# Attention scores in a mixture-of-experts block: q and k in two f32r parts on half the rows, in place of three bf16 parts on 96

## The chip, the cores and the metric

The kernel runs on one core of one Trainium2 chip. The metric is device time in microseconds, of which the median over the runs is compared. The core's engines are called PE (matrix multiplication), DVE (vector), ACT (scalar, activations), POOL (GpSimd) and SP (it only issues transfers here). SBUF has 128 partitions, and PSUM has banks of 512 f32 values in each partition.

## What is computed

One transformer layer with normalisation behind each part, for 8 sequences of 512 tokens and 256 channels: causal attention with 16 heads of 16 channels, then an expert layer in which each of 8 experts picks 129 tokens of each sequence.

```python
def proj(W):
    return jnp.einsum('btc,oc->bto', x, W).reshape(b, t, h, hd).transpose(0, 2, 1, 3) * inv_sqrt_c
k = proj(W_key)
q = proj(W_query)
v = proj(W_value)
scores = jnp.einsum('bhqd,bhkd->bhqk', q, k) * hd ** (-0.5)
causal = jnp.tril(jnp.ones((t, t), dtype=bool))
scores = jnp.where(causal, scores, -jnp.inf)
weight = jax.nn.softmax(scores, axis=-1)
out = jnp.einsum('bhqk,bhkd->bhqd', weight, v)
...
x = _layernorm(x + _L0_attn_ref(x, ...), axis=-1)
x = _layernorm(x + _L0_ffn_ref(x, ...), axis=-1)
```

The picks of the experts hang on small differences between scores, so the attention is computed nearly to f32. All inputs and outputs are f32.

## The kernel before

`attention` does the first half and `experts` the second; the change touches `attention` and the order of the weight columns in `kernel`. Each engine walks through the same list, `steps()`, and does the entries that are its own; semaphores keep the engines together. The list has 40 steps for a sequence (four quarters `g` of ten steps `k`). Each step has one `st` unit, and the `nat` units of a head group are spread over the ten steps of a quarter, three quarters ahead. In steps 4 to 7 of a quarter an `av` entry follows. The table `STAGES` puts the other work at fixed steps: `qk` (four tiles of q and k, for the sequence after next), `stack`, `nmcut` and `nm`, `v`, `onorm`, `ot`, `proj`, and the normalisation.

Scores are computed twice. The first pass, `nat` (L712), has queries in the partitions and finds each row's maximum: PE writes a bank `n_ps` (ring of 3), and DVE adds the causal mask and reduces it in one operation (L569). The second pass, `st` (L698), has keys in the partitions: PE writes `st_ps` (ring of 2) with the maximum already subtracted, ACT takes the exponential into `pt` (L485), POOL zeroes what the mask hides (L425), and `av` (L741) multiplies by v for four heads, each in its own 32 columns of the array.

To keep f32 accuracy with bf16 operands, q and k are each written as three bf16 parts that add up to the value. A score is then six products, stacked along the contraction: part `K_PARTS[i]` of k meets part `Q_PARTS[i]` of q in rows 16 i to 16 i + 15, so that 96 rows of the array (`KQ`) hold six products of 16 channels. For the second pass three rows more (`KM` = 99) hold ones on the side of k and the three parts of the negative maximum on the side of q.

The parts are made and stacked in this way. PE makes a tile of q or k (L758, f32r, six matmuls of 512 columns). ACT writes the first part (L510) and an f32 copy (L511); POOL makes the other parts with three subtractions (L434 to L436), or DVE for the first sequence (L580 to L582). SP writes the three parts to DRAM, 128 KB each (`part_d`, L362), and, once all are there, reads them into the stacks `kst` and `qst` in 12 transfers for each half of the heads (L373), since each block of 16 rows takes one. The maxima are cut into three parts by DVE (`nmcut`, L599 to L602), turned by PE (L786), copied by ACT (L523) and put into the three rows by a transfer that ACT issues (L525).

The stacks use the memory of the experts' first weights, and the parts that of the raw weights, so the trace calls them `w_parts` and `w_raw`.

## Time and profile before

| | |
|---|---|
| median of 3 runs | 932.88 us (932.07 to 934.78) |
| profiled execution | 932.33 us, span 930.6 us, mean granted TensorE clock 0.956 |
| first matmul of the experts' part, by the chain | about 483 us |
| one sequence in the middle of the attention part | 50.3 us |

The rows in the section below are read as follows. A row of the busy table has the stretch, its length, then for each engine the busy time in it and the count of instructions, then the granted clock (1.00 is 2.4 GHz), the share of DMA time and GB/s. A row of the timeline or the chain has start and duration in microseconds, engine, line and operation; "x8" behind it counts merged instructions. The duration of a matmul includes its way through the array, so what it costs the next one is the distance from start to start. One plain f32 matmul is two instructions, one f32r or bf16 matmul is one. "99x384" is 99 rows by 384 columns; "99x384 bf16 x2" in the timeline is a unit of 384 and 128 columns. PEld is the loading of the stationary operand.

### The profile page before, as it was taken

What the parts mean: (1) busy time and instruction counts of PE and PEld (TensorE: products, weight loads), DVE (VectorE), ACT (ScalarE), POOL (GpSimd) and SP (SyncE); (2) the same over time, 40 slices, a digit from 0 to 9 for tenths busy, and PEclk for the clock granted to TensorE, in tenths of its full rate; (3) what the DMA queues carried; (4) which work ended last, traced back from release to release, by engine and by line L of the source; (5) the groups of instructions that cost most, each with busy time, mean ns of one, the idle gap of its engine ahead of it and who ended that gap; (6) DMA issues with size and microseconds to landing.
All of it is one profiled execution on the core that took longest, in us unless ns stands there. A gap on an engine that the chain in (4) does not pass through costs nothing.

```text
span 930.6 us, 17149 instructions
## 1 busy us (share of the span) xinstructions
PE 822.0 (88%) x5876; PEld 616.8 (66%) x5876; DVE 604.5 (65%) x2059; ACT 532.7 (57%) x1042; POOL 472.9 (51%) x642
## 2 busy tenths in 40 slices
PE   4668999999999999988739779999999999999990
PEld 3434445454545454434339769999999999999990
DVE  4358778878788788899656863556455454646454
ACT  2226666767585767666728333656565655655555
POOL 6336666656656565332577317454443443535343
PEclk9778999999999999999979899999999999999995
DMA  4999677868586958620133404334334252513158
GB/s 139 165 151 159 103 149 124 168 93 163 112 157 120 150 108 151 157 70 3 64 108 114 121 13 69 81 92 89 76 55 124 46 138 35 143 30 54 27 137 259
DMA packets 89990, 100.52 MB, mean 108 GB/s; under 512 B 8624, under 2 KB 83376, under 8 KB 89776
## 3 DMA queue, kind: packets, MB, share of 16 engines
q1 hardware_dynamic: 72448, 77.92, 40.0%
q0 software_dynamic: 12800, 16.92, 11.2%
q10 hardware_dynamic: 4656, 4.59, 1.5%
q8 instruction: 47, 0.77, 0.4%
q14 instruction: 39, 0.32, 0.1%
HBM read 65.38 MB, written 33.62 MB: 106 GB/s over the span
## 4 chain that ended last, share of the span: by engine, by line
PE 66%; DVE 14%; ACT 5%; issue 5%; DMA 5%; POOL 2%; SPq 1%; ACTq 0%; POOLq 0%; DVEq 0%
PE y_ps L1303 19%; PE h_ps L1289 19%; PE av_ps L741 7%; DVE n_ps L569 5%; PE st_ps L709 5%; PE n_ps L724 4%; DMA part_d<-w_raw 3%; PE stage_ps L758 3%; PE stage_ps L766 3%; PE stage_ps L800 2%; PE tp_ps L1262 2%; ACT pt L485 1%; DVE nmax L569 1%; ACT res L533 1%; PE stage_ps L791 1%
## 5 line engine op out<-in xcount | busy, mean ns | idle before, releaser
L569 DVE CUSTOM_DVE_ANT_0 n_ps<-n_ps,tri 128x512 f32<-128x512 f32 (+3 forms) x512 | 238.6, 518 | 85.0 <-PE n_ps L724 83.2
L485 ACT ACTIVATE pt<-st_ps 128x512 f32<-128x512 f32 x320 | 184.3, 602 | 66.1 <-PE st_ps L709 50.8
L1303 PE MATMUL y_ps<-w_parts,h_hi 128*128 128x256 f32 (+1 forms) x1152 | 215.2, 281 | 0.6 <-DVE w_parts L1214 0.6
L1131 ACT ACTIVATE g<-h_ps,b 128x384 f32<-128x384 f32 (+1 forms) x192 | 104.3, 543 | 169.5 <-PE h_ps L1289 169.5
L1289 PE MATMUL h_ps<-tt_hi,w_parts 128*128 128x384 f32 (+1 forms) x768 | 173.1, 328 | 22.0 <-DVE tt_lo L1177 14.1
L1103 POOL DMA_INDIRECT acc<-y,tok_no x64 | 103.2, 1613 | 146.4 <-DVE y L1238 140.0
L1303 PEld LDWEIGHTS y_ps<-w_parts,h_hi 128*128 128x128 f32 (+1 forms) x1152 | 172.8, 178 | 4.2 <-ACT h_hi L1136 0.9
L425 POOL TENSOR_SCALAR_AFFINE_SELECT pt<-pt 128x256 f32<-128x256 f32 (+1 forms) x320 | 110.7, 363 | 116.6 <-ACT pt L485 115.9
L1224 DVE TENSOR_TENSOR h_lo<-g,h_hi 128x384 fp32r<-128x384 f32 (+1 forms) x176 | 90.2, 513 | 121.2 <-ACT h_hi L1136 121.0
L1303 PE MATMUL y_ps<-w_parts,h_lo 128*128 128x256 f32 (+1 forms) x576 | 161.6, 281 | 0.0
L1289 PEld LDWEIGHTS h_ps<-tt_hi,w_parts 128*128 128x128 f32 x768 | 127.9, 191 | 22.9 <-ACT tt_hi L1122 14.3
L709 PE MATMUL st_ps<-w_parts 99*128 99x512 bf16 (+3 forms) x512 | 125.2, 306 | 15.1 <-ACT pt L485 13.4
L724 PE MATMUL n_ps<-w_parts 96*128 96x512 bf16 (+3 forms) x512 | 126.2, 310 | 10.7 <-DVE nmax L569 6.9
L1303 PEld LDWEIGHTS y_ps<-w_parts,h_lo 128*128 128x128 f32 (+1 forms) x576 | 102.1, 177 | 2.1
L709 PEld LDWEIGHTS st_ps<-w_parts 99*128 99x128 bf16 x512 | 41.4, 98 | 86.8 <-ACT pt L485 56.8
L1136 ACT ACTIVATE h_hi<-g 128x384 fp32r<-128x384 f32 (+1 forms) x192 | 94.4, 492 | 7.4
L741 PE MATMUL av_ps<-pt,vaug 128*32 128x512 f32 (+3 forms) x1024 | 97.0, 453 | 0.0
L1289 PE MATMUL h_ps<-tt_lo,w_parts 128*128 128x384 f32 (+1 forms) x384 | 92.9, 323 | 0.0
L1076 POOL DMA_INDIRECT tok<-x,tok_no x58 | 58.5, 1009 | 40.0 <-issue 40.0
L569 DVE DVE_READ_ACCUMULATOR2_ANT nmax<- 128x1 f32 x512 | 71.9, 140 | 0.0
L724 PEld LDWEIGHTS n_ps<-w_parts 96*128 96x128 bf16 x512 | 44.4, 99 | 40.9 <-DVE nmax L569 25.4
L1235 DVE TENSOR_TENSOR y<-y_ps,b 128x256 f32<-128x256 f32 (+1 forms) x72 | 30.3, 421 | 58.6 <-PE y_ps L1303 54.6
...
## 6 DMA issues: line engine op xcount, KB each, us to landing
...
```

The source lines that it names most:

```text
L425: nc.gpsimd.affine_select(out=x, in_=x, compare_op=ALU.is_ge, fill=0.0, base=0, pattern=[[0, len(tiles)], [1, P]], channel_multiplier=-1). ...
L485: nc.scalar.activation(pt[:, slot % PT_RING, n % UP, :], st_ps[at % ST_RING][:, :], ACT.Exp, scale=S_SCALE).then_inc(exp_done, 1)
L569: ins = nc.vector.tensor_tensor_reduce(out=src[:, h, :], in0=src[:, h, :], in1=mask, scale=-1.0, scalar=-BIG_NEG, op0=ALU.add, op1=ALU.min ...
L709: ins = nc.tensor.matmul(st_ps[at % ST_RING][:, c:c + T - kb * P], kst[0:KM, b % 2, h, kb * P:(kb + 1) * P], qst[0:KM, b % 2, h, kb * P:T] ...
L724: ins = nc.tensor.matmul(bank[:, j * w:(j + 1) * w], qst[0:KQ, b % 2, h, qb * P:(qb + 1) * P], kst[0:KQ, b % 2, h, 0:w], start=True, stop= ...
L741: ins = nc.tensor.matmul(av_ps[VW * j:VW * (j + 1), n * P:T], vaug[:, seq % 3, n, h, :], pt[:, (seq * PAIRS + h // 2) % PT_RING, u, c:c + ...
L1103: nc.gpsimd.indirect_dma_start(acc_d[0:reach(j), :], bass.IndirectOffsetOnAxis(ap=choice(e, j), axis=0), y[0:rows_of(j), j, :], None, comp ...
L1131: nc.scalar.activation(g[:, at % G_RING, 0:cols], h_ps[at % H_RING][:, 0:cols], ACT.Gelu, bias=b1[:, e, n:n + 1]).then_inc(g_done, 1)
L1136: nc.scalar.activation(h_hi[:, q % 2, n, 0:cols], g[:, at % G_RING, 0:cols], ACT.Copy).then_inc(g_hi, 1)
L1224: nc.vector.tensor_tensor(h_lo[:, q % 2, n, 0:cols], g[:, at % G_RING, 0:cols], h_hi[:, q % 2, n, 0:cols].bitcast(F32), ALU.subtract).then ...
L1289: ins = nc.tensor.matmul(h_ps[at % H_RING][:, 0:cols], w[e % 2][:, k, units], x[:, q % TOK_RING, k, 0:cols], start=i == 0, stop=i == len(t ...
L1303: ins = nc.tensor.matmul(y_ps[at % Y_RING][0:rows, 0:C], x[:, q % 2, m, toks], w[e % 2][:, m, :], start=i == 0, stop=i == len(terms) - 1)
```

## The change

The three bf16 parts become two f32r parts, and six products become three: k in parts (0, 1, 0) against q in parts (0, 0, 1). That is 48 rows, or 50 with the two rows for the maximum. Heads are placed in two groups of rows, 0 to 49 and 64 to 113: pair n (heads 2n and 2n + 1) goes to group n mod 2. The columns of the q and k weights are put in the order in which a tile of 128 channels falls into the two groups (`HEAD_ORDER`). The `nat` units are cut anew: a pair has five units of 512 columns at most, as `st` has, and the pair is the neighbour (`slot ^ 1`) of the one that `st` has at the same place in the list, so that the two lie in different groups.

```diff
-K_PARTS = (0, 0, 1, 1, 0, 2)
-Q_PARTS = (0, 1, 0, 1, 2, 0)
-
-BLOCKS = len(K_PARTS) + len(Q_PARTS)
+K_PARTS = (0, 1, 0)
+Q_PARTS = (0, 0, 1)
+
+GROUP = P // 2
+BLOCKS = 2 * (len(K_PARTS) + len(Q_PARTS))
 KQ = len(K_PARTS) * D
-KM = KQ + 3
+KM = KQ + 2
+
+
+def place_of(h):
+
+    return h // 2 % 2, h // 4 * 2 + h % 2
+
+
+def rows_for(h, rows):
+
+    first = place_of(h)[0] * GROUP
+    return slice(first, first + rows), place_of(h)[1]
+
+
+HEAD_ORDER = [8 * n + 4 * quarter + 2 * group + h for n in range(2) for group in range(2) for quarter in range(2) for h in range(2)]
...
-N_UNITS = [(qb, h - heads + 1, heads) for h in range(H) for qb, heads in ((3, 1), (2, 1), (1, 2), (0, 4)) if (h + 1) % heads == 0]
+N_PAIR = (((0, 3, 0),), ((1, 3, 0),), ((0, 2, 0), (0, 0, 384)), ((1, 2, 0), (1, 0, 384)), ((0, 1, 0), (1, 1, 256)))
+N_UNITS = [[(2 * (slot ^ 1) + h, qb, c) for h, qb, c in unit] for slot in range(PAIRS) for unit in N_PAIR]
...
+        sp.wait_ge(ones_ready, 1)
+        for first in (0, GROUP):
+            dst = kst_b[first + KQ:first + KM, :, :, :].rearrange("p a h n -> p (a h) n")
+            sp.dma_start(dst, ones[:, :].bitcast(BF16).unsqueeze(1).to_broadcast([KM - KQ, 2 * HH, 2 * T])).then_inc(ones_in, 16)
...
-                for part in range(3):
-                    sp.dma_start(part_d[which, b % 2, part, half_, :, :], parts[:, tile % 2, part, :]).then_inc(parts_out[tile % 2], 16)
+                for part in range(2):
+                    sp.dma_start(part_d[which, b % 2, part, half_, :, :], parts[:, tile % 2, part, :].bitcast(BF16)).then_inc(parts_out[tile % 2], 16)
...
                     for at, part in enumerate(blocks):
-                        src = part_d[which, b % 2, part, n, :, :].rearrange("(h d) n -> d h n", d=D)
-                        sp.dma_start(stack[at * D:(at + 1) * D, b % 2, HH * n:HH * (n + 1), :], src).then_inc(stack_in[n][b % 2], 16)
+                        for first in (0, GROUP):
+                            src = part_d[which, b % 2, part, n, first:first + GROUP, :].rearrange("(h d) n -> d h n", d=D)
+                            sp.dma_start(stack[first + at * D:first + (at + 1) * D, b % 2, HH // 2 * n:HH // 2 * (n + 1), :],
+                                         src).then_inc(stack_in[n][b % 2], 16)
...
-                link(nc.gpsimd.tensor_tensor(qk_r[:, :], qk_f[:, tile % 2, :], parts[:, tile % 2, 0, :], ALU.subtract))
-                link(nc.gpsimd.tensor_tensor(parts[:, tile % 2, 1, :], qk_f[:, tile % 2, :], parts[:, tile % 2, 0, :], ALU.subtract))
-                nc.gpsimd.tensor_tensor(parts[:, tile % 2, 2, :], qk_r[:, :], parts[:, tile % 2, 1, :], ALU.subtract).then_inc(qk_rest, 1)
+                nc.gpsimd.tensor_tensor(parts_r[:, tile % 2, 1, :], qk_f[:, tile % 2, :], parts[:, tile % 2, 0, :], ALU.subtract).then_inc(qk_rest, 1)
...
-                act.dma_start(qst[KQ:KM, b % 2, HH * n:HH * (n + 1), :], nmt[:, :]).then_inc(rows_in, 16)
+                for group in range(2):
+                    act.dma_start(qst_b[group * GROUP + KQ:group * GROUP + KM, b % 2, HH // 2 * n:HH // 2 * (n + 1), :],
+                                  nmt[HH * group:HH * (group + 1), :].bitcast(BF16)).then_inc(rows_in, 16)
...
-                link(nc.vector.tensor_copy(nm3[:, :, 0, :], mine))
-                link(nc.vector.tensor_tensor(nmax_r[:, :, :], mine, nm3[:, :, 0, :], ALU.subtract))
-                link(nc.vector.tensor_copy(nm3[:, :, 1, :], nmax_r[:, :, :]))
-                nc.vector.tensor_tensor(nm3[:, :, 2, :], nmax_r[:, :, :], nm3[:, :, 1, :], ALU.subtract).then_inc(nm_parts, 1)
+                link(nc.vector.tensor_copy(nm2[:, :, :, 0, :].bitcast(F32R), mine))
+                nc.vector.tensor_tensor(nm2[:, :, :, 1, :].bitcast(F32R), mine, nm2[:, :, :, 0, :], ALU.subtract).then_inc(nm_parts, 1)
...
                 for hh, kb, c in ST_UNITS[u]:
-                    h = 2 * pair + hh
-                    ins = nc.tensor.matmul(st_ps[at % ST_RING][:, c:c + T - kb * P], kst[0:KM, b % 2, h, kb * P:(kb + 1) * P],
-                                           qst[0:KM, b % 2, h, kb * P:T], start=True, stop=True)
+                    rows, slot = rows_for(2 * pair + hh, KM)
+                    ins = nc.tensor.matmul(st_ps[at % ST_RING][:, c:c + T - kb * P], kst[rows, b % 2, slot, kb * P:(kb + 1) * P],
+                                           qst[rows, b % 2, slot, kb * P:T], start=True, stop=True)
...
-                for j in range(heads):
-                    h = h0 + j
-                    ins = nc.tensor.matmul(bank[:, j * w:(j + 1) * w], qst[0:KQ, b % 2, h, qb * P:(qb + 1) * P],
-                                           kst[0:KQ, b % 2, h, 0:w], start=True, stop=True)
+                for h, qb, c in N_UNITS[n]:
+                    w = (qb + 1) * P
+                    rows, slot = rows_for(h, KQ)
+                    ins = nc.tensor.matmul(n_ps[at % N_RING][:, c:c + w], qst[rows, b % 2, slot, qb * P:(qb + 1) * P],
+                                           kst[rows, b % 2, slot, 0:w], start=True, stop=True)
```

On PE the order moves a little. Where `st`, `nat`, `av` and the matmuls of `v` take turns (in steps 5 to 7 of the third quarter), it reads before (L709 `st`, L724 `nat`, L741 `av`, L766 `v`):

```order
324 L709 MATMUL st_ps<-w_parts 128x384
325 L709 MATMUL st_ps<-w_parts 128x128
326 L724 MATMUL n_ps<-w_parts 128x384
327 L741 MATMUL av_ps<-pt,vaug 32x256 x4
328 L766 MATMUL stage_ps<-w_hi,xt_hi 128x264 x2
329 L766 MATMUL stage_ps<-w_hi,xt_lo 128x264 x2
330 L766 MATMUL stage_ps<-w_lo,xt_hi 128x264 x2
331 L709 MATMUL st_ps<-w_parts 128x256 x2
332 L724 MATMUL n_ps<-w_parts 128x512
```

and after (L725 `st`, L739 `nat`, L756 `av`, L781 `v`):

```order
350 L725 MATMUL st_ps<-w_parts 128x384
351 L725 MATMUL st_ps<-w_parts 128x128
352 L739 MATMUL n_ps<-w_parts 128x512
353 L756 MATMUL av_ps<-pt,vaug 32x256 x4
354 L781 MATMUL stage_ps<-w_hi,xt_hi 128x264 x2
355 L781 MATMUL stage_ps<-w_hi,xt_lo 128x264 x2
356 L781 MATMUL stage_ps<-w_lo,xt_hi 128x264 x2
357 L725 MATMUL st_ps<-w_parts 128x256 x2
358 L739 MATMUL n_ps<-w_parts 128x384
359 L739 MATMUL n_ps<-w_parts 128x128
```

The places of all operations stay. The `nat` unit beside each `st` unit has other columns, and every step has one, where before 11 units fell on ten steps.

On POOL the tiles of q and k stand between the masks of `pt`. Before (L425 mask, L434 to L436 split):

```order
56 L425 AFFINE_SELECT pt<-pt 128x2x128 x2
57 L434 TENSOR_TENSOR w_raw<-w_raw 128x512
58 L435 TENSOR_TENSOR w_raw<-w_raw 128x512
59 L436 TENSOR_TENSOR w_raw<-w_raw 128x512
60 L425 AFFINE_SELECT pt<-pt 128x128
```

and after (L450 mask, L459 split):

```order
63 L450 AFFINE_SELECT pt<-pt 128x2x128 x2
64 L459 TENSOR_TENSOR w_raw<-w_raw 128x512
65 L450 AFFINE_SELECT pt<-pt 128x128
66 L450 AFFINE_SELECT pt<-pt 128x2x128
67 L450 AFFINE_SELECT pt<-pt 128x128
```

Two of three subtractions are gone. On ACT, where the turned maxima are stored, there stands before:

```order
68 L485 ACTIVATE pt<-st_ps 128x512 x6
69 L523 ACTIVATE nmt<-stage_ps 24x512
70 L525 DMA w_parts<-nmt 3x8x512
71 L485 ACTIVATE pt<-st_ps 128x512
72 L492 ACTIVATE xt_hi<-w_raw 128x1024
```

and after:

```order
68 L503 ACTIVATE pt<-st_ps 128x512 x6
69 L541 ACTIVATE nmt<-stage_ps 16x512
70 L544 DMA w_parts<-nmt 2x4x1024 x2
71 L503 ACTIVATE pt<-st_ps 128x512
72 L510 ACTIVATE xt_hi<-w_raw 128x1024
```

ACT issues two transfers there, one for each group of rows.

## Rows read from the trace of the kernel before

**Rows 1.** The page: busy time of each engine, and the chain by engine.

```profile
PE 822.0 (88%) x5876; PEld 616.8 (66%) x5876; DVE 604.5 (65%) x2059; ACT 532.7 (57%) x1042; POOL 472.9 (51%) x642
PE 66%; DVE 14%; ACT 5%; issue 5%; DMA 5%; POOL 2%; SPq 1%; ACTq 0%; POOLq 0%; DVEq 0%
```

**Rows 2.** Busy table of middle sequences; PE, PEld, DVE, ACT, POOL, clock, DMA share, GB/s.

```profile
194.12:244.44 50.32, 48.25 (x354) 25.53 (x353) 40.18 (x168) 34.61 (x71) 31.09 (x57) 1.00 0.77 138
294.72:345.03 50.31, 48.22 (x354) 25.52 (x353) 40.18 (x168) 34.62 (x71) 31.08 (x57) 1.00 0.73 127
```

**Rows 3.** Timeline of PE, separate steps around `av`; start, us, engine, line.

```profile
264.07 0.39 PE L709 MATMUL st_ps<-w_parts 99*128 99x384 bf16 x2
264.30 0.33 PE L724 MATMUL n_ps<-w_parts 96*128 96x384 bf16 x1
264.56 0.64 PE L741 MATMUL av_ps<-pt,vaug 128*32 128x256 f32 x8
265.13 0.39 PE L709 MATMUL st_ps<-w_parts 99*128 99x256 bf16 x2
265.36 0.38 PE L724 MATMUL n_ps<-w_parts 96*128 96x512 bf16 x1
```

**Rows 4.** Timeline of PE where steps follow each other directly.

```profile
258.96 0.39 PE L709 MATMUL st_ps<-w_parts 99*128 99x256 bf16 x2 [0.37 <-ACT pt L485]
259.25 0.39 PE L724 MATMUL n_ps<-w_parts 96*128 96x512 bf16 x1
```

**Rows 5.** Weight loads by form, 150 to 350 us: busy us, mean ns, idle before.

```profile
L724 PEld LDWEIGHTS n_ps<-w_parts 96*128 96x128 bf16 x255 | 22.0, 97 | 9.6 <-DVE nmax L569 4.6
L758 PEld LDWEIGHTS stage_ps<-xt_hi,w_hi 128*128 128x128 f32 x32 | 5.3, 189 | 2.7 <-DVE scores L617 1.3 <-ACT o_t L529 0.8
```

**Rows 6.** Timeline of PE: four f32 transposes, then a step with six `nat` matmuls.

```profile
276.66 0.60 PE L750 MATMUL stage_ps<-ident,av_sb 128*128 128x128 f32 x4
277.10 0.38 PE L709 MATMUL st_ps<-w_parts 99*128 99x384 bf16 x2
277.32 0.60 PE L724 MATMUL n_ps<-w_parts 96*128 96x256 bf16 x6
277.76 0.38 PE L709 MATMUL st_ps<-w_parts 99*128 99x512 bf16 x1
```

**Rows 7.** The chain in order of time, in the experts: f32r matmuls of 256 columns.

```profile
650.25 2.84 PE y_ps L1303 x24
```

**Rows 8.** Timeline of PE: `av` of 128 columns, then `v`.

```profile
254.37 0.43 PE L741 MATMUL av_ps<-pt,vaug 128*32 128x128 f32 x8
254.73 0.51 PE L766 MATMUL stage_ps<-w_hi,xt_hi 128*128 128x264 f32 x2
255.07 0.41 PE L766 MATMUL stage_ps<-w_hi,xt_lo 128*128 128x264 f32 x2
255.31 0.40 PE L766 MATMUL stage_ps<-w_lo,xt_hi 128*128 128x264 f32 x2
```

**Rows 9.** Timeline of ACT: the issue of the transfer of the maxima.

```profile
263.47 0.73 ACTq L525 DMA_DIRECT2D w_parts<-nmt  x1
```

**Rows 10.** Groups of DVE, 150 to 350 us: the second cast of the maxima.

```profile
L601 DVE CAST nm<-nmax_r 128x32 bf16<-128x32 f32 x8 | 5.2, 651 | 0.3
```

**Rows 11.** Waits, 150 to 350 us: us in total, times, longest.

```profile
PEld n_ps L724 <- DVE nmax L569: 4.6, 20, 0.3
```

**Rows 12.** The chain in order of time, at the start.

```profile
17.82 0.70 DVE w_raw L581
...
28.57 8.84 DMA part_d<-w_raw
...
38.73 1.18 POOL w_raw L434
```

**Rows 13.** Busy table of the first 50 us, columns as in rows 2.

```profile
0.00:50.00 50.00, 28.24 (x107) 20.41 (x107) 22.28 (x59) 11.50 (x23) 24.60 (x27) 0.86 0.79 151
```

**Rows 14.** Timeline of PE: the first `av`.

```profile
85.15 1.07 PE L741 MATMUL av_ps<-pt,vaug 128*32 128x512 f32 x8
```

77 lines of the change are left out of this document (37 added, 40 removed).

## The prediction

> **What bounds the kernel now.** I read the page first: PE is busy 88% of the span and two thirds of the chain that ended last are PE work [rows 1]. The second half of that chain is the experts (`h_ps`, `y_ps`), which the change does not touch. Then I read the four middle sequences of the attention part with the busy table by windows [rows 2]: each takes 50.3 us, with PE busy 48.2, DVE 40.2, ACT 34.6 and POOL 31.1. So PE is the bound, DVE comes next with 10 us to spare, and the clock was granted in full (1.00, the 2.4 GHz level), so durations there can be added without a correction. The timeline of PE then shows what a step of the loop costs [rows 3]: one `st` unit and one `nat` unit, 512 columns each at most, then usually something else (`av`, `v`, `qk`, `proj`, a transpose). A step's `st` unit runs 0.22 to 0.23 us and so does a `nat` unit of 512 columns: 0.42 ns a column, one column a cycle at 2.4 GHz. Forty steps of two units are 17.6 us of the 50.3.
>
> About 26 of the 40 steps of a sequence have another PE operation ahead of their `st` unit (193 such places stand in the whole program's order, over eight sequences with shorter ends). I call these **separate** steps. The other 14 follow each other directly; there `st` waits for the exponentials of ACT [rows 4] and a quicker PE would mostly wait longer. So the separate steps decide.
>
> **What the change can gain.** In the order of the new program a `st` unit of one head pair stands beside a `nat` unit of the other pair, which lies on the other half of the rows. Only neighbours in PE's order can overlap, and PE takes matmuls in order, so within a separate step it is the last `st` matmul that can run beside the first `nat` matmul. The five kinds of step, with s for one column at 0.42 ns, need at best: 512 beside 512, 0.21 us; 384, then 128 beside 512, 0.37; 256, then 256 beside 384, then 128, 0.32; 512 beside 384 and 128, 0.21; 384, then 128 beside 256 and 256, 0.37. Mean 0.30 instead of 0.44.
>
> **What loads take of it.** The operands turn from bf16 to f32r. The f32 loads of 128 columns have a mean of 189 ns where the bf16 ones have 97 [rows 5], and where short operations follow each other, four f32 transposes take 0.44 us, 0.11 each [rows 6]; six bf16 matmuls (2 x 256, 4 x 128 columns) took 0.44 right behind them [rows 6], which is their 1024 columns and nothing more, so bf16 loads never showed. The f32r matmuls of 256 columns in the experts take 2.84 us for 24, 0.118 each [rows 7], against 0.107 for the columns. A load of 128 f32r columns is thus worth up to 0.11 to 0.12 us of PE, and I take 0.11. A step has two to four loads (3.2 on average), so 0.35 us, more than the 0.30 above. With the first load out of the way, each further one 0.11 us later, the five kinds take 0.32, 0.43, 0.43, 0.32 and 0.43 us; mean 0.386, a gain of 0.054 a step. The Trainium skill, TensorE: Matmul & The Clock Gate, section LDWEIGHTS, gives columns / 1.2 ns for a load, 107 ns for 128, and no dependence on rows: half the rows would load no faster. The rows of the trace agree with that for f32, and by it the sum is the same.
>
> **What entering and leaving the half-row arrangement costs.** The trace has one change of the array's arrangement: from 128 x 128 to the four 32-column strips of `av`. There a `nat` unit of 384 columns lasts 0.26 us until `av` starts, where its columns take 0.16 [rows 3]: 0.10 us. On the way back, the first two `v` matmuls take 0.34 us behind `av` where the next two take 0.24 [rows 8]: another 0.10. No row shows a change to half the rows. Its bounds: nothing, if the next loads run under what is still streaming, as they do now between `v` and `st`; and 0.19 us, a whole f32 load [rows 5], if nothing is loaded ahead. A bf16 load that was not ahead cost 0.07 (0.29 instead of 0.22, where `st` waited for ACT [rows 4]). I take 0.13, the middle of 0.07 and 0.19, since the array's one rearrangement that the trace shows is not free. The Trainium skill, TensorEngine Tiling (Array Packing), section Key Properties, says that changing the tiling mode drains TensorE. The `av` rows agree; without a drain the sum would be that of the second case below.
>
> So a separate step costs 0.386 + 0.13 = 0.516 instead of 0.44: 26 x 0.076 = **+2.0 us** a sequence. Ten steps leave for an f32 operation over all rows (in the others `av` follows, which is paid already): 10 x 0.10 = **+1.0 us**.
>
> **The rest of a sequence.** ACT issues two transfers of the row maxima where it issued one, 0.73 us each [rows 9]. The first of the two places lies where the exponentials hold PE, so one of them is paid: **+0.7 us**; the other is under PE work. DVE loses two of the four operations of `nmcut` (the cast of 0.65 us [rows 10] and a subtraction of 0.19, for each half), some 1.7 us a sequence, and its units now come one a step instead of 11 for ten steps; PE's loads wait 4.6 us for DVE in four sequences [rows 11], so I take **-0.8 us** of the 1.15 a sequence. POOL loses two subtractions of 1.18 us (as in [rows 12]) for each of four tiles, 9.4 us a sequence, but no PE wait on POOL is long there, so nothing. The stacks take as many transfers of 128 KB as before (12 a half), in lines of 2 KB instead of 1; the parts go out as two transfers of 256 KB instead of three of 128, a third more bytes. The queue has gaps in every sequence (DMA share 0.73 to 0.77 [rows 2]), so nothing either.
>
> Sum for one sequence: 2.0 + 1.0 + 0.7 - 0.8 = **+2.9 us**. PE is the bound in about six of eight: from 95 to 388 us (293 / 50.3 = 5.8); behind that the picking rounds stand on DVE, and I count nothing there. 6 x 2.9 = +17.4 us.
>
> **The start.** The first 85 us are a chain through the parts: a tile of q or k is split (DVE 0.70 us three times for the first, POOL 1.18 three times later), written out (8.84 us from issue to landing, behind the transfers ahead of it), and read back [rows 12]. One of three subtractions stays. On the chain stand one DVE group and three POOL groups: 2 x 0.72 + 3 x 2 x 1.2 = 8.6 us go. But what is late next is the transfers, busy 0.79 of the first 50 us [rows 13], whose bytes grow. Bounds: 0 and -8.6; I take half, **-4.3 us**.
>
> **The number.** The profiled execution took 932.33 us with a span of 930.6; the median of the three runs is 932.88, so I count from 932.3 and lose nothing that matters. 932.3 + 17.4 - 4.3 = **945 us**, slower by 1.4%.
>
> **Rivals.**
> (a) *Loads go ahead of the change* (faster, a little). If entering costs nothing, a step gains 0.054: -1.4 + 0.7 - 0.8 = -1.5 a sequence, -9 in six, with the start 932.3 - 9 - 4.3 = **919 us**. For it: between `v` and `st` nothing is lost now. Against: the `av` rows. The point between this and my forecast is an entry of about 0.07 us.
> (b) *Full overlap* (faster, clearly). If loads to the idle half hide, a step takes 0.30: -0.14 x 26 = -3.6, with the other terms -3.7; six times -22, and the start: **906 us**. For it: the four strips of `av` do run together, since four heads of 256 plain f32 columns take 0.57 us [rows 3] and of 128 take 0.36 [rows 8], 0.21 for 128 columns more, which is four cycles a column once and not four times over. Against: the f32 load row. The Trainium skill, TensorE: Matmul & The Clock Gate, section Measured speedup vs the span model, has a pack of tiles take one matmul plus 4 ns for each further one: that is this case. It would end at DVE's 40 us only if it gained ten.
> (c) *Narrow f32r is slow* (slower still). Sixteen `st` and sixteen `nat` matmuls a sequence have 128 columns. No f32r row in the trace is under 256 columns. Bounds: one cycle a column as at 264 (0.24 for two [rows 8]), or four, as plain f32 in `av` (0.21 for 128 [rows 3, 8]). At four, 0.16 us more where the narrow one ends a step (two kinds in five): 0.064 x 26 = 1.7, times six +10: **955 us**.
> (d) *The halves don't run together.* Then the step stays at 0.44, pays the entry and some 0.04 for f32r (0.118 against 0.107, 3.2 times): +0.17 x 26 = 4.4, a sequence +5.3, six +32: **960 us**.
>
> **How the numbers follow.** Forecast 0.28, (a) 0.25, (b) 0.22, (c) 0.15, (d) 0.07, something else 0.03. The entry's own bounds (0.07 to 0.19) move the forecast by 9 us each way, 936 to 954. The range goes from 905, to hold (b)'s centre, to 958, past (c). A measurement of this kernel tells 0.3% (2.8 us) from no change: faster 0.44 ((a) but for a small part, and (b)), within 0.3% 0.07, slower 0.49.
>
> **What would show it.** After, a `st` unit behind `v` or `proj` starts later, by 0.1 us or more, than the last matmul before it allows; at nothing, (a) or (b). From `st` start to the next operation's start, a 512 + 512 step takes 0.32 us in the forecast and in (a), 0.21 to 0.25 in (b), 0.43 in (d). The 128-column matmuls show (c). A middle sequence would take 53 us; 46.6 is (b). The start shows in when the first `av` begins (85.15 us now [rows 14]). Wrong I would be most simply if loads of one half run fully under matmuls of the other.

## The result, and the profile after

The kernel after takes 970.92 us (median of 4 runs, 968.14 to 975.86) where the kernel before took 932.48 beside it (4 runs, 931.38 to 934.78): a ratio of 1.0415, interval 1.0361 to 1.0468. The change costs 38 us, more than the range of the prediction allowed (905 to 958). The profiled execution took 975.86 us.

The page of the kernel after: its span, its busy times, and its clock in 40 slices.

```profile
span 974.1 us, 17037 instructions
PE 874.2 (90%) x5876; PEld 663.5 (68%) x5876; DVE 587.5 (60%) x2019; ACT 533.7 (55%) x1042; POOL 405.3 (42%) x585
PEclk9557899898989899896687988999999999999996
```

The same row of the page of before reads

```profile
PEclk9778999999999999999979899999999999999995
```

PE is busy 52 us longer [rows 1], and the clock row says why to look further than at the operations. Behind a first 9 it reads 5, 5, 7, 8, then 9 with an 8 at about every second slice, then 6, 6 in the nineteenth and twentieth, where the kernel before had 9 in all slices of the middle. To place the loss I cut both executions at the same points of the program: at the start of ACT's cast `xt_hi` in the fourth and in the eighth `split`, and at the first `h_ps` matmul, with which the experts begin. The busy table by windows (columns as in [rows 2]), before:

```profile
0.00:113.57 113.57, 80.44 (x423) 48.10 (x427) 65.72 (x241) 44.84 (x94) 59.52 (x81) 0.86 0.84 147
113.57:315.09 201.52, 192.93 (x1416) 102.10 (x1408) 161.02 (x669) 138.47 (x281) 124.35 (x224) 1.00 0.75 137
315.09:482.93 167.84, 137.72 (x1019) 66.45 (x1012) 139.06 (x551) 102.29 (x193) 84.97 (x170) 0.95 0.42 89
482.93:930.60 447.67, 410.93 (x3030) 400.12 (x3030) 238.74 (x601) 247.08 (x477) 204.04 (x167) 0.96 0.40 92
```

and after:

```profile
0.00:120.61 120.61, 96.28 (x429) 62.52 (x429) 59.61 (x231) 44.95 (x93) 35.47 (x64) 0.73 0.75 153
120.61:338.77 218.16, 203.88 (x1412) 114.69 (x1408) 157.43 (x653) 139.18 (x281) 90.05 (x192) 0.91 0.65 137
338.77:525.85 187.08, 161.82 (x1017) 85.18 (x1010) 131.88 (x536) 102.21 (x193) 76.23 (x162) 0.82 0.37 82
525.85:974.10 448.25, 412.22 (x3030) 401.07 (x3030) 238.62 (x601) 247.33 (x477) 203.57 (x167) 0.96 0.40 92
```

The experts take the same time to 0.6 us. The attention part loses 7.0 us at its start, 16.6 in four middle sequences and 19.2 in its last stretch, and in each the clock is lower. The clock has two levels here, so a mean of 0.91 over 218 us is 2 x 0.09 x 218 = 39 us at the lower one. From here on **half clock** is the time at 1.2 GHz, summed as 2 x (1 - clock) over windows of 1 us. The three stretches have 31, 0 and 16 us of it before, 65, 38 and 69 us after.

The timeline of PE shows both what the change gained and what it paid. Two steps of the kernel after at full clock follow (start, us, engine, line). Behind the first, at 263.15, another step comes directly; the second is a separate one, between `v` and `av`:

```profile
263.15 0.49 PE L725 MATMUL st_ps<-w_parts 50*128 50x512 f32 x1
263.15 0.51 PE L739 MATMUL n_ps<-w_parts 48*128 48x384 f32 x2
263.48 0.34 PE L725 MATMUL st_ps<-w_parts 50*128 50x384 f32 x1
...
267.26 0.41 PE L781 MATMUL stage_ps<-w_lo,xt_hi 128*128 128x264 f32 x2
267.60 0.44 PE L725 MATMUL st_ps<-w_parts 50*128 50x384 f32 x1
267.61 0.50 PE L739 MATMUL n_ps<-w_parts 48*128 48x512 f32 x1
267.88 0.22 PE L725 MATMUL st_ps<-w_parts 50*128 50x128 f32 x1
268.03 0.64 PE L756 MATMUL av_ps<-pt,vaug 128*32 128x256 f32 x8
```

`st` and `nat` begin within 0.01 us of each other, and the next step begins 0.33 us after the first. In the second step `nat`'s only matmul starts 0.27 us ahead of `st`'s second one, so it runs beside both. The two halves do run together. The Trainium skill, TensorE: Matmul & The Clock Gate, section Measured speedup vs the span model, gives a pack one matmul plus about 4 ns for each further tile. The trace agrees on the starts (at most 0.01 us apart) and not on the length: the step takes 0.33 us, where 512 columns alone take 0.22.

A separate step of 512 beside 512 columns, from the start of `st` to that of the next operation, takes 0.43 us all the same, hardly less than before (192.24 to 192.68, 0.44 us):

```profile
204.30 0.50 PE L725 MATMUL st_ps<-w_parts 50*128 50x512 f32 x1
204.30 0.49 PE L739 MATMUL n_ps<-w_parts 48*128 48x512 f32 x1
204.73 1.16 PE L815 MATMUL stage_ps<-wp,o_t 128*128 128x264 f32 x4
```

That is 0.33 us for the step and 0.10 for leaving the half rows.

The last `v` pair, 528 columns, lasts 0.34 us until `st` starts; 0.10 us of that is the change to half the rows, since the same pair ahead of another `v` takes 0.24 [rows 8], and ahead of `st` on 99 rows it took 0.25 in the kernel before, from 255.31 to

```profile
255.56 0.39 PE L709 MATMUL st_ps<-w_parts 99*128 99x512 bf16 x1
```

And the kernel after some 20 us later, at half clock (note `qk`, line 773, whose pairs take 0.46 to 0.57 us to the next at full clock and 1.01 here):

```profile
286.00:290.00 4.00, 3.87 (x14) 2.79 (x15) 3.01 (x12) 2.21 (x4) 2.77 (x8) 0.54 0.62 175
```
```profile
288.05 1.22 PE L773 MATMUL stage_ps<-xt_hi,w_hi 128*128 128x512 f32 x2
289.06 1.05 PE L773 MATMUL stage_ps<-xt_lo,w_hi 128*128 128x512 f32 x2
```

So there were three candidates for the loss: the loads and changes of arrangement, which the forecast had counted; new waits; and the clock, which it had not counted.

### The profile page after: what moved, and what is told of

It reads as the page before. It is cut to its first block, busy times and chain, and to the rows that moved or that the text cites. A ratio compares the mean times of both kernels' runs of the same rounds, so it can differ in the third digit from the quotient of the medians.

```text
span 974.1 us, 17037 instructions
## 1 busy us (share of the span) xinstructions
PE 874.2 (90%) x5876; PEld 663.5 (68%) x5876; DVE 587.5 (60%) x2019; ACT 533.7 (55%) x1042; POOL 405.3 (42%) x585
## 4 chain that ended last, share of the span: by engine, by line
PE 78%; ACT 8%; issue 5%; DVE 3%; DMA 3%; POOL 1%; SPq 1%; ACTq 1%; POOLq 0%; DVEq 0%
PE y_ps L1318 18%; PE h_ps L1304 18%; PE st_ps L725 10%; PE av_ps L756 9%; PE stage_ps L773 6%; PE stage_ps L815 4%; PE n_ps L739 4%; ACT pt L503 3%; PE stage_ps L781 3%; PE stage_ps L765 2%; PE tp_ps L1277 2%; PE stage_ps L801 1%; PE stage_ps L806 1%; ACT res L553 1%; DMA w_parts<-part_d 1%
## 5 line engine op out<-in xcount | busy, mean ns | idle before, releaser
L450 POOL TENSOR_SCALAR_AFFINE_SELECT pt<-pt 128x256 f32<-128x256 f32 (+1 forms) x320 | 112.6, 361 | 207.5 <-ACT pt L503 205.8
L725 PE MATMUL st_ps<-w_parts 50*128 50x512 f32 (+3 forms) x512 | 163.7, 397 | 28.0 <-ACT pt L503 26.4
L1304 PE MATMUL h_ps<-tt_hi,w_parts 128*128 128x384 f32 (+1 forms) x768 | 173.4, 328 | 16.6 <-ACT tt_hi L1137 9.3
L739 PE MATMUL n_ps<-w_parts 48*128 48x512 f32 (+3 forms) x512 | 168.6, 412 | 4.0 <-DMA w_parts<-part_d 2.7
L725 PEld LDWEIGHTS st_ps<-w_parts 50*128 50x128 f32 x512 | 88.5, 204 | 118.7 <-ACT pt L503 66.0
L756 PE MATMUL av_ps<-pt,vaug 128*32 128x512 f32 (+3 forms) x1024 | 109.9, 507 | 0.0
L739 PEld LDWEIGHTS n_ps<-w_parts 48*128 48x128 f32 x512 | 92.3, 214 | 13.0 <-issue 6.7
L1304 PEld LDWEIGHTS h_ps<-tt_lo,w_parts 128*128 128x128 f32 x384 | 67.8, 192 | 0.0
```

The lines of the kernel that those rows point to most:

```text
L450: nc.gpsimd.affine_select(out=x, in_=x, compare_op=ALU.is_ge, fill=0.0, base=0, pattern=[[0, len(tiles)], [1, P]], channel_multiplier=-1). ...
L725: ins = nc.tensor.matmul(st_ps[at % ST_RING][:, c:c + T - kb * P], kst[rows, b % 2, slot, kb * P:(kb + 1) * P], qst[rows, b % 2, slot, kb ...
L739: ins = nc.tensor.matmul(n_ps[at % N_RING][:, c:c + w], qst[rows, b % 2, slot, qb * P:(qb + 1) * P], kst[rows, b % 2, slot, 0:w], start=Tr ...
L756: ins = nc.tensor.matmul(av_ps[VW * j:VW * (j + 1), n * P:T], vaug[:, seq % 3, n, h, :], pt[:, (seq * PAIRS + h // 2) % PT_RING, u, c:c + ...
L1304: ins = nc.tensor.matmul(h_ps[at % H_RING][:, 0:cols], w[e % 2][:, k, units], x[:, q % TOK_RING, k, 0:cols], start=i == 0, stop=i == len(t ...
```

## The experiments

One note ahead of the texts on record. The half-clock times in the expectations were read from the clock's record with its times counted from another zero, which lies about 11 us ahead of the span's start (11.1 in the kernel after), so each sum covers a stretch that lies 11 us too early. Those in my text and in the table are counted from the span's start, and agree with the durations of the matmuls. For four middle sequences the two readings are 34.1 and 37.5 us for the kernel after, 54.6 and 51.2 for e3, 20.5 and 17.1 for e9. No verdict turns on the difference.

Where in an execution the clock is low is known for one of each kernel, the profiled one. Its mean over the whole is known for every run, and the kernels differ by more than their runs do: 0.945 to 0.956 before, 0.894 to 0.905 after, 0.864 and 0.870 in e3, 0.917 twice in e9, 0.931 and 0.923 in e10.

### e1 and e2: without the overlap; with all rows

e1 puts the two units of a step on the same half:

```diff
-N_UNITS = [[(2 * (slot ^ 1) + h, qb, c) for h, qb, c in unit] for slot in range(PAIRS) for unit in N_PAIR]
+N_UNITS = [[(2 * slot + h, qb, c) for h, qb, c in unit] for slot in range(PAIRS) for unit in N_PAIR]
```

> The changed kernel with the nat unit taken from the same head pair as the st unit beside it, so both lie on the same half of the rows and cannot overlap; all else as in the changed kernel. In the changed kernel the clock is granted at about 0.90 in a middle sequence, where it was 1.00 before. Theory R (matmuls on half the rows hold the clock up less, whatever their order): the clock stays at 0.85 to 0.92 in the middle. Theory I (the overlap makes PE finish early and wait, and the waits let the clock fall): the clock goes back to 1.00. In both a separate step grows from 0.43 us to about 0.6, if the overlap was real, and by 25 steps a sequence at full clock gets some 4 us longer than the changed kernel's, total 985 to 1010 us under R, 960 to 980 under I.

e2 runs every score matmul over all 128 rows of the f32r stacks (the rows between and behind the groups are filled with zeros by transfers at the start):

```diff
-    return slice(first, first + rows), place_of(h)[1]
+    return slice(0, P), place_of(h)[1]
...
-                                     scale=S_SCALE).then_inc(exp_done, 1)
+                                     scale=S_SCALE * 1e-3).then_inc(exp_done, 1)
```

> The changed kernel with every score matmul over all 128 rows of the same f32r stacks: the unused rows are set to zero once at the start, the other group's head is added into each score, and the exponential's scale is a thousandth, so the attention weights come out wrong; number, width and order of all operations are the changed kernel's. No overlap, no rearrangement of the array. Theory R and theory I: the clock is 1.00 in the middle. A separate step then costs what it did before plus at most 0.05 us for f32r; a middle sequence 50 to 52 us. If f32r alone lowered the clock it would stay near 0.90. The start has 1.8 MB more to transfer, so the total is read from the middle sequences only; expected total 935 to 950 us.

e1 took 1088.63 us in its profiled run and 1111.8 in its other one, so it has no interval; the kernel before took 932.76 beside it. e2 took 962.29 us, ratio 1.0314 (1.0284 to 1.0344). Two middle sequences of e1 and one of e2, busy table, columns as above:

```profile
121.22:198.03 76.81, 75.29 (x346) 44.38 (x342) 39.84 (x163) 36.16 (x72) 22.70 (x48) 0.68 0.48 97
198.03:262.31 64.28, 63.34 (x357) 38.42 (x353) 40.34 (x163) 35.75 (x72) 22.73 (x48) 0.85 0.56 116
```
```profile
237.49:289.84 52.35, 50.80 (x353) 34.77 (x352) 39.42 (x164) 34.57 (x71) 22.53 (x48) 1.00 0.68 142
```

Without the overlap the kernel is 113 us slower than with it (1088.63 against 975.86, the profiled runs). By their mean clocks, 0.823 and 0.894, e1 has about 178 us more at half clock; at the price below that is an estimated 77 of the 113 us, and the rest is the overlap itself. The clock fell further than Theory R had it (0.68 to 0.85 in the middle, where it expected 0.85 to 0.92), and the time lies above its range.

In e1 PE is busy 98% of the time and waits for almost nothing, and yet 20 to 49 us of each sequence are at half clock: new waits are not the cause of the low clock there. In e2, with the same f32r operands and loads, the middle sequences have 1.00 again. Its sequence is 2.1 us longer than before's 50.3: that is the price of f32r, with its other edits of the sequence (the maxima in two parts, two transfers of rows), and no change to half the rows. The total missed its forecast of 935 to 950 us, mainly by the start: the middle begins at 132.73 us instead of 113.57, behind the added transfers.

The sequences of one kernel with different clocks also price the clock: (76.81 - 64.28) us for (49.0 - 19.9) us more at half clock, 0.43 us for each. By the same price a sequence of e1 would take 64.28 - 0.43 x 19.9 = 55.7 us at full clock.

### e3, e4, e9, e10: rows alone, in the kernel before

These four leave the stacks, the loads and the `nat` units of before as they are (bf16) and only read fewer rows; the products of the rows left out are missing, in e3, e9 and e10 the maximum too. The edit of e3 for both passes:

```diff
-                    ins = nc.tensor.matmul(st_ps[at % ST_RING][:, c:c + T - kb * P], kst[0:KM, b % 2, h, kb * P:(kb + 1) * P],
+                    ins = nc.tensor.matmul(st_ps[at % ST_RING][:, c:c + T - kb * P], kst[0:KQ // 2, b % 2, h, kb * P:(kb + 1) * P],
...
-                    ins = nc.tensor.matmul(bank[:, j * w:(j + 1) * w], qst[0:KQ, b % 2, h, qb * P:(qb + 1) * P],
+                    ins = nc.tensor.matmul(bank[:, j * w:(j + 1) * w], qst[0:KQ // 2, b % 2, h, qb * P:(qb + 1) * P],
```

That is rows 0 to 47 in both passes. e4 reads rows 64 to 98 for `st` and 0 to 47 for `nat`, so on opposite halves; e9 reads rows 0 to 63 in both passes, e10 rows 0 to 67.

> The kernel before (bf16, three parts) with both passes' score matmuls cut to rows 0 to 47: three of six products and the subtraction of the maximum are left out, all else is unchanged. Half the rows without f32r and without overlap. Theory R: the clock falls in the middle sequences to about 0.90 as in the changed kernel, total 955 to 980 us. Theory I: the clock stays 1.00; the cost is the rearrangement alone, some 0.1 us for each of 26 entries and 10 exits, a sequence of 52 to 54 us, total 945 to 960 us.

> The kernel before with the nat matmuls on rows 0 to 47 and the st matmuls on rows 64 to 98 (the last two products and the maximum), so that neighbours lie on opposite halves in bf16: products are left out of the scores. The overlap of the changed kernel with the quicker bf16 loads. If loads limit a step (my prediction), a separate step falls from the 0.32 of the changed kernel (to the last matmul's end) to about 0.27, since a bf16 load is 0.05 us shorter. Theory R and theory I: the clock is below 1.00, 0.85 to 0.92; total 945 to 965 us, below the changed kernel by 10 us or more through the loads.

> The kernel before (bf16) with both passes' score matmuls cut to rows 0 to 63: four of six products, no subtraction of the maximum. 64 rows still fit half of the array. Run beside the same kernel with 68 rows. With 48 rows there were 7 to 20 us a sequence at half clock. Theory R, by the count of rows: a little better than with 48 rows, 3 to 14 us a sequence at half clock, 960 to 1000 us. Theory S (the arrangement on half the array and the changes into and out of it let the clock fall, not the rows): as with 48 rows, 1000 to 1020 us.

> The same with rows 0 to 67, four more rows, which takes the matmuls over all of the array without any rearrangement; the rows that hold data are nearly as few as in the run with 64. Theory R: nearly the clock of the run with 64 rows, well below 1.00 in the middle, total within 15 us of it (the changes themselves cost 3 us a sequence). Theory S: the clock is back at 1.00 in the middle as with 96 rows, 930 to 940 us.

Measured: e3 1013.4 us, ratio 1.0862 (1.0796 to 1.0928); e4 946.63, 1.0146 (1.0117 to 1.0175); e9 976.7, 1.0464 (1.0411 to 1.0516); e10 945.76, 1.0132 (1.0038 to 1.0226). Middle sequences of e3, e4, e9 and e10 in the busy table, the one at the highest clock and the one at the lowest of each:

```profile
244.41:297.77 53.36, 51.66 (x362) 24.67 (x363) 40.78 (x168) 34.85 (x72) 31.14 (x56) 1.00 0.70 127
297.77:360.81 63.04, 61.24 (x352) 27.53 (x344) 41.03 (x168) 34.79 (x72) 31.30 (x56) 0.81 0.61 112
```
```profile
216.75:268.83 52.08, 47.83 (x346) 22.89 (x344) 40.00 (x167) 34.55 (x71) 31.02 (x56) 0.90 0.75 133
268.83:319.06 50.23, 46.80 (x364) 22.31 (x363) 40.95 (x169) 34.54 (x71) 30.97 (x56) 0.97 0.73 138
```
```profile
120.65:177.43 56.78, 54.97 (x350) 25.60 (x346) 40.92 (x167) 34.86 (x71) 31.12 (x56) 0.91 0.66 122
231.88:285.33 53.45, 51.74 (x365) 24.73 (x363) 40.77 (x168) 34.93 (x72) 31.08 (x56) 1.00 0.72 127
```
```profile
113.30:165.18 51.88, 49.79 (x360) 26.48 (x352) 40.17 (x168) 34.61 (x71) 31.05 (x56) 0.97 0.73 130
267.61:317.89 50.28, 48.20 (x360) 25.53 (x352) 40.18 (x169) 34.61 (x71) 30.96 (x56) 1.00 0.76 138
```

Two costs come apart here. **The arrangement:** at full clock 48 and 64 rows take 53.4 us, 68 rows take 50.3, as before does with 96. Rows in number change nothing; an arrangement of half the rows costs 3.1 us a sequence, in bf16. The timeline of e9 shows a piece of it; `qk`'s last pair takes 0.55 us until `st` here and 0.46 in e2 (210.69 to 211.15), where all rows are used:

```profile
257.84 0.62 PE L758 MATMUL stage_ps<-xt_hi,w_lo 128*128 128x512 f32 x2
258.39 0.39 PE L709 MATMUL st_ps<-w_parts 64*128 64x512 bf16 x1
```
```profile
210.69 0.62 PE L777 MATMUL stage_ps<-xt_hi,w_lo 128*128 128x512 f32 x2
211.15 0.39 PE L728 MATMUL st_ps<-w_parts 128*128 128x512 f32 x1
```

**The clock:** with the work otherwise equal, half clock in four middle sequences is 0, 6.8, 17.1 and 51.2 us for 96, 68, 64 and 48 rows. PE is busy 96 to 97% of the time in all four, and the mean clocks of all their runs stand in the same order. So fewer rows lower the clock, with no f32r, no overlap and no other part of the change: from 96 to 68 rows without the cost of another arrangement (50.3 us in both), from 64 to 48 rows with the same cost. Whether the arrangement lowers the clock too is not separated. Between 64 and 68 rows it goes, and 10 us of half clock with it, where four rows are a small step.

Neither theory had the sizes. e3 lies above Theory R's 955 to 980 us, and e10 lies 31 us below e9, where R had at most 15, and above the 930 to 940 of Theory S.

The overlap in bf16 is e4 against e3: e4's four sequences, brought to full clock at 0.34 us for each us, come to 48.4 to 49.3 us, against 53.4: a gain of 4 to 5 us. The overlap gives clock back as well: e4 has 23.9 us of half clock in four sequences where e3 has 51.2, and with f32r the kernel after has 37.5 where e1 has 144.8.

### e8: half rows, loads as bf16

The kernel after, but the score matmuls read the upper 16 bits of each element of the same stacks:

```diff
-kst[rows, b % 2, slot, kb * P:(kb + 1) * P]
+kst_b[rows, b % 2, slot, 2 * kb * P + 1:2 * (kb + 1) * P:2]
```

> The changed kernel with the score matmuls reading the upper 16 bits of each f32r value as bf16 (every second bf16 element of the same stacks), so the parts lose accuracy; rows, widths, order and overlap are the changed kernel's, and only the operand type of the score matmuls differs. If the f32r load (0.11 us before the first matmul of a separate step) is what f32r costs, a separate step falls from 0.43 us to 0.37 to 0.38 and a middle sequence by 25 x 0.05 = 1.3 us plus what the clock gives. Theory R: the clock is still gated, 5 to 14 us a sequence at half clock; total 945 to 968 us. If f32r has its own part in the clock: 1.00 in the middle and 925 to 935 us.

939.73 us (4 runs), ratio 1.0072 (1.0031 to 1.0113). Two steps and their surroundings:

```profile
247.51 0.40 PE L725 MATMUL st_ps<-w_parts 50*128 50x512 bf16 x1
247.51 0.40 PE L739 MATMUL n_ps<-w_parts 48*128 48x384 bf16 x2
247.75 0.33 PE L725 MATMUL st_ps<-w_parts 50*128 50x384 bf16 x1
...
251.35 0.41 PE L781 MATMUL stage_ps<-w_lo,xt_hi 128*128 128x264 f32 x2
251.69 0.34 PE L725 MATMUL st_ps<-w_parts 50*128 50x384 bf16 x1
```

A step of 512 beside 512 columns takes 0.24 us where f32r took 0.33, so 0.09 us of an f32r load shows in each, and the overlap itself is nearly perfect (512 columns alone are 0.22). The entry behind `v` stays at 0.34 us: it does not depend on the type. With the operand type of the score matmuls alone, 31 of the 38 us are gone, and the time lies below Theory R's 945 to 968. The four middle sequences are 12.7 us shorter (205.44 against 218.16), 3.2 each. About 0.9 of that is 2.6 us less of half clock; the other 2.3 are 26 separate steps x 0.09. The start and the last stretch give more than the middle (8.4 and 16.0 us in the profiled executions), with less half clock too (41.0 us in place of 54.6 in the first 85 us, 48.1 in place of 68.9 in the last stretch); how much of that is loads and how much clock is not separated.

### e5 and e6: fillers where the steps follow each other

In the 15 direct steps of a sequence one matmul of 512 f32r columns is put ahead of `st`, on all rows (e5) or on 64 (e6); it writes a bank that the next `nat` unit overwrites.

```diff
+FILL_AT = (0, 1, 2, 4, 10, 12, 13, 14, 24, 30, 31, 32, 33, 34, 39)
...
+                    nc.tensor.matmul(n_ps[bank % N_RING][:, :], w_hi[0:P, 0, 0:P], w_hi[0:P, 0, 0:T], start=True, stop=True)
```

> The changed kernel with one more matmul of 512 columns over all 128 rows (q weights by q weights, the result is overwritten by the nat unit of the same step) ahead of the st unit in the 15 steps of a sequence whose st follows directly on nat. There PE mostly waits for ACT. Theory R (half-row matmuls do too little to hold the clock): the clock goes up in the middle, half-clock time falls from the 6.8 to 10.2 us a sequence of the changed kernel to 0 to 3.4; a middle sequence falls from 52 to 56 us to 49 to 51; total 935 to 955 us. Theory S (each change between whole and half rows lets the clock fall): the filler adds 15 changes each way, the clock falls more, total 975 to 1000 us.

> The same filler matmuls as in the run with all rows, in the same 15 places, but over 64 rows (the half on which the nat unit of that step lies). Same columns, so PE is as busy by time. If the clock asks only how busy PE is, it recovers as with all rows (0 to 3.4 us at half clock a sequence). Theory R: it recovers little, 5 us or more at half clock a sequence, and the total stays at 960 to 985 us. Theory S: no added changes, the total is that of the changed kernel, 965 to 980.

e5: 982.43 us, 1.0532 (1.0453 to 1.0611). e6: 967.6 us, 1.0373 (1.0335 to 1.041), by its time not told apart from the kernel after. e6 did what Theory R had for it. e5, which should have had a better clock than e6, did not, and missed R's 935 to 955 us; it lies in the range of Theory S, but through the columns of the fillers, as the end of this section shows. What led to them is where the clock falls. In the kernel after it fell at the same two places of nearly every middle sequence, some 47 us and some 4 us behind its start. Around 276 and 286 us the busy table reads

```profile
272.00:276.00 4.00, 2.55 (x21) 1.67 (x20) 3.48 (x15) 3.67 (x10) 1.12 (x4) 1.00 0.21 80
276.00:280.00 4.00, 4.00 (x21) 1.80 (x22) 3.07 (x17) 2.35 (x5) 1.38 (x4) 0.57 0.48 165
...
283.00:286.00 3.00, 1.85 (x19) 1.06 (x19) 1.78 (x9) 3.00 (x7) 2.23 (x2) 1.00 0.01 4
286.00:290.00 4.00, 3.87 (x14) 2.79 (x15) 3.01 (x12) 2.21 (x4) 2.77 (x8) 0.54 0.62 175
```

and the kernel before, over the same part of the program, does not fall:

```profile
257.00:261.00 4.00, 3.34 (x23) 1.55 (x21) 3.57 (x19) 4.00 (x11) 1.27 (x5) 1.00 1.13 152
...
264.80:268.00 3.20, 2.68 (x30) 1.14 (x23) 2.32 (x10) 3.20 (x7) 2.37 (x2) 1.00 0.22 75
```

Ahead of each fall PE works through direct steps at ACT's pace (ACT is busy 4.00 us of 4.00 in the kernel before and 3.67 in the kernel after). The overlapped steps are done sooner and leave PE idle 0.4 to 0.6 us between two of them: 2.55 us busy of 4 and 1.85 of 3, where before had 3.34 of 4 and 2.68 of 3.2. Over the middle, `st` waits for ACT 14.1 us instead of 6.4. The same row of e8 stands third:

```profile
PE st_ps L725 <- ACT pt L503: 14.1, 29, 0.6
```
```profile
PE st_ps L709 <- ACT pt L485: 6.4, 20, 0.4
```
```profile
PE st_ps L725 <- ACT pt L503: 18.7, 31, 0.7
```

The Trainium skill, TensorE: Matmul & The Clock Gate, section A second HAM failure mode: psum-queue depth-cycling, describes short idle times of PE between groups of matmuls that keep the clock going up and down. These rows have that form, with gaps of at most 0.6 us.

But from kernel to kernel the half clock does not follow these waits. e8 waits more than the kernel after (18.7 us) and has less of it, 27.3 us. e1 waits only 4.3 us over its four sequences and has the most, 144.8.

With the fillers the fall at 47 us is gone in both kernels; the one at 4 us stays. Half clock in four middle sequences is 27.3 us in both, from 37.5, and the mean clock of every run is above that of the kernel after (0.910 to 0.926 in e5, 0.911 to 0.921 in e6, 0.894 to 0.905 after). So work in the gaps helps. That full and half rows do the same in it speaks for the gaps and not for the rows; since e8 has the same 27.3 us without fillers, the gaps are argued as a cause and not shown. Each filler of e5 costs what it streams: its sequence at full clock took 54.41 us, 3.3 more than after's 51.1 (below), and 15 x 0.22 = 3.3.

### e11 and e12: each half filled up to 64 rows

Both put zeros into rows 48 to 61 of each half and move the maxima and the ones to rows 62 and 63; e12 also has e8's edit. `st` reads all 64 rows and `nat` 62; the expectation has the two the wrong way round.

```diff
+TOP = GROUP - 2
...
-                    rows, slot = rows_for(2 * pair + hh, KM)
+                    rows, slot = rows_for(2 * pair + hh, GROUP)
...
-                    rows, slot = rows_for(h, KQ)
+                    rows, slot = rows_for(h, TOP)
```

> The kernel after, with each half of the stacks filled up from 50 to 64 rows: the parts stay in rows 0 to 47, rows 48 to 61 hold zeros in both stacks, the maxima and the ones move to rows 62 and 63; the second pass reads rows 0 to 61, the first rows 0 to 63. The result is the same; four memsets on GpSimd at the start are added, off the chain as I read it. Theory R (the chip goes by the rows that a matmul addresses, whatever is in them): in the kernel before, cutting the rows from 96 to 68, 64 and 48 gave 0, 6.8, 20.4 and 54.6 us at half clock in the four middle sequences; so 62 and 64 rows in place of 48 and 50 take half-clock time there from 34 us to 14 or less, the last stretch before the experts from 34 us down by some 10 as well, and the time to about 950 us (940 to 958). Rival D (it goes by rows that carry data, or by the partial results that change): zero rows do nothing, half-clock time stays at 30 to 38 us in the four sequences and the time at 966 to 976 us.

> Both edits in one: 64 rows in each half filled up with zeros as in e11, and the score matmuls read the upper 16 bits of every element as bf16, as in e8 (which leaves out the lower bits of the parts). e8 alone: 939.7 us, 27.3 us at half clock in four sequences of 51.3 us. Theory R: half-clock time there falls to 10 or less, each sequence by 2 to 3 us to about 49, six sequences and a quieter start give 15 to 20 us, so 920 to 927 us, under the kernel before (933). Rival D (zero rows do nothing): 936 to 943 us as in e8.

e11: 963.7 us (4 runs), 1.0336 (1.029 to 1.0381), against 1.0415 (1.0361 to 1.0468) for the kernel after. e12: 937.62 us (10 runs), 1.0045 (1.0026 to 1.0063), against e8's 1.0072 (1.0031 to 1.0113). Half clock in four middle sequences fell from 37.5 to 20.5 us in e11, from 27.3 to 20.5 in e12. The rows that are addressed count, at least in part, though they hold only zeros. Rival D falls by e11's clock, whose mean is 0.910 to 0.914 in its four runs against 0.894 to 0.905 after; the time alone lies between the two forecasts, and e11's interval touches that of the kernel after. e12 settles nothing by itself: its time lies in the range of rival D (936 to 943), and its mean clocks (0.919 to 0.930) overlap with e8's (0.908 to 0.922). Theory R was right in direction and took too much: the clock did not come back wholly, and e12 doesn't beat the kernel before. One sequence of e12 ran at full clock throughout:

```profile
116.34:165.01 48.67, 43.65 (x352) 20.43 (x352) 38.87 (x163) 34.35 (x71) 22.42 (x48) 1.00 0.76 154
216.59:268.00 51.41, 46.47 (x352) 21.58 (x352) 38.88 (x163) 34.47 (x72) 22.44 (x48) 0.93 0.70 146
```

48.67 us is less than before's 50.3: with bf16 loads and at full clock the arrangement would gain 1.6 us a sequence. The later one, the same work, takes 2.7 us more for 6.8 us at half clock.

### e7: the new cut of the `nat` units alone

The kernel before, with only one part of the change: `nat` units by pair, five of 512 columns at most (`N_PAIR` as in the change, and each unit walked through as a list).

```diff
-N_UNITS = [(qb, h - heads + 1, heads) for h in range(H) for qb, heads in ((3, 1), (2, 1), (1, 2), (0, 4)) if (h + 1) % heads == 0]
+N_UNITS = [[(2 * slot + h, qb, c) for h, qb, c in unit] for slot in range(PAIRS) for unit in N_PAIR]
```

> The kernel before with the changed kernel's cut of the nat units alone (five of at most 512 columns for each pair, one a step; bf16, 96 rows, three parts as before). It prices the term of -0.8 us a sequence that I gave to evener units: 927 to 930 us if it holds, 932 if DVE's waits only move, with the clock at 1.00 in the middle in both.

928.95 us (6 runs, 928.15 to 930.29) beside 933.49 (10 runs): 0.9955 (0.9938 to 0.9972), a little faster than the kernel before, as expected, though by less than 0.5%. Its middle sequences take 50.0 to 50.3 us at 1.00, 0.3 us less each, so the term of -0.8 us a sequence was too large; the rest of the 4.5 us lies outside the middle. The evener units are the part of the change that is worth keeping.

## Why the prediction was wrong

At one clock the books close. Sequences of one kernel with different amounts of half clock price it: 0.34 us for each us in the kernel after ((55.84 - 52.35) / (13.7 - 3.4)), about 0.40 in e3 and e12, 0.43 in e1 and e5. Pairs with little half clock between them give 0.28 (e11) to 0.47 (e10), so the second digit of a price is not to be trusted. The four middle sequences:

| kernel | rows, type | us each | half clock us each | one at full clock |
|---|---|---|---|---|
| before | 96/99, bf16 | 50.3 to 50.6 | 0 | 50.3 |
| e10 | 68, bf16 | 50.3 to 51.9 | 0, 3.4 | 50.3 |
| e9 | 64, bf16 | 53.5 to 56.8 | 0, 3.4, 3.4, 10.2 | 53.4 |
| e3 | 48, bf16 | 53.4 to 63.0 | 0, 8.1, 19.2, 23.9 | 53.4 |
| e4 | 48 + 35 on two halves, bf16 | 50.2 to 52.1 | 3.5, 3.8, 6.6, 10.1 | about 49 |
| e2 | 128, f32r | 52.4 | 0 | 52.4 |
| e1 | 48/50, f32r, same half | 64.3 to 76.8 | 19.9, 37.9, 37.9, 49.0 | about 55.7 |
| after | 48/50, f32r, two halves | 52.4 to 55.8 | 3.4, 10.2, 10.3, 13.7 | about 51.1 |
| e8 | 48/50, bf16, two halves | 51.2 to 51.6 | 6.8 each | about 48.9 |
| e11 | 62/64, f32r, two halves | 52.4 to 53.4 | 3.4, 3.4, 6.8, 6.8 | about 51.1 |
| e12 | 62/64, bf16, two halves | 48.7 to 51.6 | 0, 6.8, 6.8, 6.8 | 48.7 |

In the column of rows, 48/50 means 48 rows in `nat` and 50 in `st`. In the last column "about" marks a value worked out with that price: 52.35 - 3.4 x 0.34 = 51.2, 50.9 at 0.43. The parts are +3.1 (arrangement: e3, e9), +2.1 (f32r: e2) and -4.6 (overlap: e1 to after; -4 to -5 from e3 to e4), together +0.6; found +0.8.

**The step that failed is the first one:** "the clock was granted in full (1.00, the 2.4 GHz level), so durations there can be added without a correction". This was true of the kernel before and was carried over to a kernel that uses half the rows, where 37.5 us of the four middle sequences were at half clock. The clock has no term in the sum, no rival and no sign of being wrong. Of the 42.9 us up to the experts, the middle's 16.6 are 4 x 0.8 = 3 at full clock and 13 by 38 us of half clock. The last stretch has 53 us more of it for 19.2 us longer, 0.36 each, the same price. The start has 34 more for 7.0 us, 0.21 each, less than the price. The experiments show that the rows bring the clock down and price it in the middle; that the whole 19.2 and 7.0 are clock is read from these prices and not shown by a run of its own. e2 comes nearest: with the same f32r operands on all rows it has 7.9 us of half clock in the last stretch and takes 168.56 us there, against 167.84 before and 187.08 after.

A second step failed with it. Of the sequences behind 388 us the prediction said "the picking rounds stand on DVE, and I count nothing there". Yet 19.2 of the 42.9 us came behind 338.77 us. From 443 to 478 us, 48 to 83 us ahead of the experts, PE of the kernel after is busy 33.63 of 35 us at half clock; over the same distance (400 to 435 us) it was busy 29.41 of 35 before. That reads as if the low clock had made PE the bound there too.

**Overlap.** "PE takes matmuls in order, so within a separate step it is the last `st` matmul that can run beside the first `nat` matmul" is wrong: `nat` starts with `st`'s first matmul and runs beside both. A step takes 0.24 us in bf16 (e8), where I had a mean of 0.30 as the best case.

**Loads.** I took 0.11 us for each further f32r load, on one chain for both halves, and so 0.386 us. Found are 0.33 and some 0.09 us over bf16: about one load shows in a step, and the others run under its matmuls. Separate steps take 0.43 us to the next operation whether they have two loads (204.30) or four (198.87 to 199.30, 256 + 256 beside 384 + 128). Rows don't make a load cheaper, as I said: 189 ns for 128 rows [rows 5], 199 and 202 ns now, over a stretch with some half clock in it:

```profile
L739 PEld LDWEIGHTS n_ps<-w_parts 48*128 48x128 f32 x233 | 39.9, 202 | 0.0
L725 PEld LDWEIGHTS st_ps<-w_parts 50*128 50x128 f32 x234 | 39.3, 199 | 54.2 <-ACT pt L503 32.0 <-issue 19.7
```

**Entering and leaving.** Taken 0.13 and 0.10, found 0.09 to 0.10 at the entry and the same on the way out: `nat` of 384 columns lasts 0.25 us until `proj` in e9 (258.62 to 258.87) and 0.16 on 68 rows in e10 (274.10 to 274.26). In a sequence that is 3.1 us where I had 26 x 0.13 + 1.0 = 4.4. That changing the arrangement isn't free was right. Together with overlap and loads the sum of a sequence came out as +2.9, found about +0.8, six of them some 12 us too much: but for the clock, the forecast would have been too high.

**The start.** The -4.3 us did not come: the first `av` starts at 87.96 instead of 85.15 [rows 14], with 54.6 us of the first 85 at half clock instead of 30.7.

**Rivals.** (b) was right that the halves run fully beside each other, wrong that the loads hide. (c) is refuted: a 128-column f32r matmul lasts 0.22 us, as in bf16. (d) did not happen. Its total was right, 50.3 + 5.3 = 55.6 us for a sequence without overlap and 55.7 in e1, but partly by luck: the arrangement was 3.1 us where (d) had 4.4, and f32r with the other edits 2.1 where it had 0.9. No rival had the clock, and the range was as wide as costs counted in columns and loads could make it.

**Left open.** What exactly lowers the clock: rows addressed act (e3, e9, e10, e11), and work in short gaps of PE helps (e5, e6). But e1 has the lowest clock with hardly a gap, e8 has longer waits and a better clock than the kernel after, and the fillers did the same on 64 as on 128 rows. The overlap of two halves raised the clock (e1 to the kernel after, e3 to e4), and no run tests what in it does so. Nor was it looked into why the stretch from 443 us stays at half clock for 34 us on end with PE 96% busy.
